# Stack rows interleaved over the partitions, and the scatters of the first batches spread over the attention's last events

## What is computed

```
def _attn(q_in, k_in, v_in, wq, bq, wk, bk, wv, bv, wo, bo, causal):
    Q = (q_in @ wq + bq).reshape(Bq, Sq, H, HD)
    Kp = (k_in @ wk + bk).reshape(Bq, Sk, H, HD)
    V = (v_in @ wv + bv).reshape(Bq, Sk, H, HD)
    scores = jnp.einsum('bqhd,bkhd->bhqk', Q, Kp) / jnp.sqrt(jnp.float32(HD))
...
    a = jax.nn.softmax(scores, axis=-1)
    o = jnp.einsum('bhqk,bkhd->bqhd', a, V).reshape(Bq, Sq, Dm)
    return o @ wo + bo
...
x = _layernorm(x + _attn(x, x, x, ..., True), ln1_g, ln1_b)
x = _layernorm(x + _attn(x, encoder_output, encoder_output, ..., False), ln2_g, ln2_b)
x = _layernorm(x + _moe(x, router_w, router_b, e_w1, e_b1, e_w2, e_b2), ln3_g, ln3_b)
```

## Time and profile before

| | |
|---|---|
| median of 3 runs | 1187.5 us (1185.99 to 1188.43) |
| the profiled execution | 1185.79 us, of which the span 1183.9 us |
| mean granted TensorE clock | 0.938 |
| busy: TensorE matmul, weight load | 1041.1 us (88%), 597.6 us (50%) |
| busy: VectorE, ScalarE, GpSimd | 558.8 us (47%), 588.9 us (50%), 306.5 us (26%) |

### The profile page before, as it was taken

How to read it: one execution, slowest core, us unless ns; L and a number is a source line. 1 busy time by engine, 2 the same in 40 slices (tenths; PEclk the granted TensorE clock), 3 DMA queues, 4 the chain that set the end, 5 groups by cost and what they waited for, 6 DMA issues and landing times. The chain is left out here.

```text
span 1183.9 us, 19018 instructions
## 1 busy us (share of the span) xinstructions
PE 1041.1 (88%) x6318; PEld 597.6 (50%) x6319; DVE 558.8 (47%) x905; ACT 588.9 (50%) x1199; POOL 306.5 (26%) x416
## 2 busy tenths in 40 slices
PE   3889889999999998998998998975429999999976
PEld 1544445333335533343432333321329999999965
DVE  2441467775665576665674754740321121111116
ACT  1246344675764575765565665654143334444422
POOL 5533532404105603003223030243021111111104
PEclk8989889999999999999999998996759999999988
DMA  7985466208209304107507042011031203323324
GB/s 191 130 125 81 69 78 75 43 2 100 37 2 132 57 2 62 20 2 105 154 1 81 1 55 27 1 55 54 30 101 53 98 27 111 106 102 115 107 86 141
DMA packets 71069, 83.41 MB, mean 70 GB/s; under 512 B 10592, under 2 KB 64608, under 8 KB 70880
## 3 DMA queue, kind: packets, MB, share of 16 engines
q1 hardware_dynamic: 63328, 63.17, 30.9%
q0 software_dynamic: 5504, 17.34, 4.6%
q10 hardware_dynamic: 2176, 2.10, 0.5%
HBM read 38.63 MB, written 12.10 MB: 43 GB/s over the span
## 5 line engine op out<-in xcount | busy, mean ns | idle before, releaser
L1101 DVE TENSOR_REDUCE max_q<-v_slot 128x1 f32<-128x1024 f32 (+3 forms) x352 | 399.7, 1172 | 185.0 <-PE v_slot L929 121.5
L1059 ACT ACTIVATE probs<-a_bank 128x512 f32<-128x512 f32 (+1 forms) x688 | 362.6, 591 | 219.8 <-PE a_bank L956 139.8
L956 PE MATMUL a_bank<-q_stack_cross,k_stack_cross 99*128 99x512 bf16 x512 | 172.9, 399 | 26.8 <-issue 11.7
L929 PE MATMUL v_slot<-k_stack_cross,q_stack_cross 96*128 96x512 bf16 x512 | 155.7, 390 | 10.0 <-DMA q_stack_cross<-parts 8.8
L1441 ACT ACTIVATE hidden<-a_bank,b 128x128 f32<-128x128 f32 x216 | 79.4, 368 | 153.2 <-PE a_bank L1389 139.2
L971 PE MATMUL o_bank<-probs,v_cross 128*32 128x512 f32 x1024 | 141.9, 627 | 9.2 <-issue 3.8
L956 PEld LDWEIGHTS a_bank<-q_stack_cross,k_stack_cross 99*128 99x128 bf16 x512 | 47.4, 99 | 167.4 <-ACT probs L1059 86.9
L1397 PE MATMUL v_slot<-stack_or_weights,hidden 128*128 128x256 f32 x576 | 130.3, 379 | 0.0
L1397 PEld LDWEIGHTS v_slot<-stack_or_weights,hidden 128*128 128x128 f32 x576 | 106.7, 190 | 13.0
L1389 PE MATMUL a_bank<-x_col,stack_or_weights 128*128 128x128 f32 x864 | 109.6, 277 | 1.6 <-issue 1.6
L1389 PEld LDWEIGHTS a_bank<-x_col,stack_or_weights 128*128 128x128 f32 x864 | 106.3, 194 | 3.8 <-issue 2.0
(11 more groups left out here) (217 smaller groups left out, 1186.1 us busy)
## 6 DMA issues: line engine op xcount, KB each, us to landing
stack_or_weights<-in_e_w SPq DMA_DIRECT2D x16, 1024.0 KB, 7.8
stack_or_weights<-parts SPq DMA_DIRECT2D x96, 128.0 KB, 5.9
k_stack_cross<-parts SPq DMA_DIRECT2D x96, 128.0 KB, 5.9
q_stack_cross<-parts SPq DMA_DIRECT2D x48, 128.0 KB, 6.4
x_slots<-slots_in SPq DMA_DIRECT2D x38, 129.0 KB
ctxt<-in_ctxT POOLq DMA_DIRECT2D x4, 1024.0 KB, 10.6
xt<-in_xT POOLq DMA_DIRECT2D x4, 512.0 KB, 6.8
xres<-in_x POOLq DMA_DIRECT2D x4, 512.0 KB, 4.4
```

Of the source, the lines that this page charges most:

```text
L929: last = nc.tensor.matmul(slot[:, half * S:(half + 1) * S], lhs, k_stack[1][0:KR, G * u + j, half * S:(half + 1) * S], start=True, stop=True)
L956: last = nc.tensor.matmul(bank[:, i * cols:(i + 1) * cols], lhs, q_stack[kind][0:KM, G * u + j, q0:S], start=True, stop=bool(kind))
L1059: nc.scalar.activation(probs[tile % 2][:, js[0]:js[-1] + 1, q0:S], a_bank[at % AS][:, 0:len(js) * (S - q0)].rearrange("p (j t) -> p j t", ...
L1101: nc.vector.tensor_reduce(most, rows, X, ALU.max, negate=True).then_inc(v_free, 1)
```

## The change

**Interleaved rows.** The row of group g and feature d of a stack moves from partition 16 g + d to partition 6 d + g. A transfer still writes 16 partitions, now every sixth one of the 96, instead of 16 neighbouring ones. Number, size and order of the transfers are the same.

**Scatters one by one.** The event `scatter` becomes 24 events, each with one indirect transfer. The first is put behind the first weighing after `place`, and one more behind each further weighing; what is left when the list ends goes to its end. The waits for slots and rows stand before the first; the wait for landing stands behind the whole list. GpSimd has no part in a weighing.

```
-        last = max(self.order.index(("max_parts", len(UNIT_LIST) - 1)), self.order.index(("place",)))
-        self.order.insert(last + 1, ("scatter",))
+
+        rows = [("scatter", t, k) for t in range(LAST_BATCH) for k in range(2)]
+        spread, started = [], False
+        for ev in self.order:
+            spread.append(ev)
+            started = started or ev == ("place",)
+            if started and ev[0] == "weigh" and rows:
+                spread.append(rows.pop(0))
+        self.order = spread + rows
...
-                                sp.dma_start(stack[g * HD:(g + 1) * HD, h0:h0 + 8, t0:t0 + S], parts[no % 2][:, part, :]).then_inc(stack_in[s], 16)
+                                sp.dma_start(stack[g:KR:NG, h0:h0 + 8, t0:t0 + S], parts[no % 2][:, part, :]).then_inc(stack_in[s], 16)
...
                 elif k == "scatter":
-                    pool.wait_ge(slots_ready, 2)
-                    pool.wait_ge(kept, NO.ln[B - 2, 1] + 1)
-                    for t in range(LAST_BATCH):
-                        for kk in range(2):
-                            pool.indirect_dma_start(out=slots_dram, out_offset=bass.IndirectOffsetOnAxis(ap=early.slot_i[:, kk, t:t + 1], axis=0),
-                                                    in_=x2_all[:, t, :], in_offset=None).then_inc(scattered, 16)
-                    pool.wait_ge(scattered, 16 * 2 * LAST_BATCH)
+                    t, kk = ev[1:]
+                    if t == 0 and kk == 0:
+                        pool.wait_ge(slots_ready, 2)
+                        pool.wait_ge(kept, NO.ln[B - 2, 1] + 1)
+                    pool.indirect_dma_start(out=slots_dram, out_offset=bass.IndirectOffsetOnAxis(ap=early.slot_i[:, kk, t:t + 1], axis=0),
+                                            in_=x2_all[:, t, :], in_offset=None).then_inc(scattered, 16)
+            pool.wait_ge(scattered, 16 * 2 * LAST_BATCH)
```

## The result

| | before | after |
|---|---|---|
| median, same job | 1187.97 us (1185.99 to 1191.55, 4 runs) | 1131.66 us (1130.4 to 1136.96, 4 runs) |
| profiled execution, its span | 1185.79 us, 1183.9 us | 1130.4 us, 1128.5 us |
| mean granted TensorE clock | 0.938 | 0.965 |

The ratio is 0.9531 (95% interval 0.9493 to 0.957). The forecast was 1139 us with a range of 1120 to 1165. Behind the changed list of events (line 172) a line of after is 7 further down than in before, the restacking's line too (L737 is L744).

What follows compares the result with a forecast made beforehand. The prediction took TensorE's own queue in the attention to set the pace. From the profiled execution, 1185.8 - 27 (gaps) - 9 (clock) - 11 (scatters) = 1138.8 us, said as 1139, range 1120 to 1165.

Steps and rivals of the forecast that it cites:

- TensorE's gaps: TensorE's waits in the attention tied to restacking transfers, 30.1 us in sum: a gain of 27 us, bounds 15 and 30.
- nearly all of it can go: Of the 30.1 us of TensorE's waits tied to restacking, each at most 4.7 us, nearly all disappears: 27 us taken.
- The transfer: A restacking transfer's landing falls from 5.9 to 2.3 us, bounded below by the output's transfer at 2.1 us.
- rivals 4 and 5: Restacking transfers get no faster, only the scatters' part gains, 1175 us (chance 0.05); or they get slower, 1231 us (chance 0.07).
- The clock: TensorE's clock falls after restacking waits would go: a gain of 9 us, bounds 3 and 15.
- seven stretches at 1.2 GHz: Stretches around TensorE's restacking waits where the clock falls to its lower level; the shortfall adds up to 37.5 us.
- the half of 37.5: Where TensorE is the limit, half of the time at the lower clock is lost: 18.7 us at most.
- The scatters in unit 31: Breaking up the run of 24 scatters beside unit 31's weighings gains 11 us of 20.8 lost, bounds 0 and 20.8.
- What I kept: Loss left in unit 31 with twelve scatters in a row: 7.1 us, and 3 for the clock.
- The end of the list: The seven late scatters' wait for landing hides behind the routing's matmuls: cost 0, up to 1 us.
- the forecast's own sign: In the profile after, the step into the second part comes no later than 0.5 us after VectorE's last logits.
- The five early scatters: Five scatters behind `place`, done before GpSimd is next needed: cost 0, up to 4 us if TensorE suffers from them.

Runs made afterwards that it cites:

- the third job: A batch of executions with before beside it at 1188.41 us (7 runs); the kernel after, run again in it unchanged, took 1133.78 us.
- the second job: A batch of executions with before beside it at 1168.88 us (9 runs), testing another spread of the rows, paced scatters and added plain transfers.
- the kernel of the second job with twelve scatters in a row: The kernel after, but restacking transfers write every second partition of a range of 32 instead of every sixth of 96: 1130.27 us (2 runs).
- the paced kernel of the third job: The kernel after, but with all 24 scatters paced by weighings, the first ones too, and none behind the last norm: 1122.51 us, ratio 0.9455.

## Why the prediction was right, and where it was off

- **TensorE's gaps: 27 us, measured 27.0** (idle time up to the last weighing of unit 30, 51.2 to 24.3). The step "nearly all of it can go" held: the waits on `parts` and `max_t` are gone and ScalarE took up little.
- **The transfer: 2.3 us, measured 2.4**, with 146 GB/s at share 0.54. The row on which it rested, the output's transfer over 128 partitions, was the right neighbour, with some luck: it differs in more than its partitions, as it is twice the size and writes to memory and not to a stack. That the partitions are what counts was shown afterwards, by the runs that change nothing else. By rivals 4 and 5 it would have stayed at 5.9 or grown.
- **The clock: 9 us, measured 20.4.** This term was mis-sized, beyond its bound of 15. I had counted seven stretches at 1.2 GHz, 37.5 us; the records of before hold ten between 30 and 788 us, 54.6 us together, and those of after two, 6.8 us. The profiled execution of the same kernel in the third job tells the parts of the miss. There all seven that I counted are gone, and the three that I hadn't (17.1 us in before) stand as they were, though the restacking waits are gone; TensorE's busy time up to the last weighing of unit 30 is 690.66 us, 16.6 less than in before. That is 0.9 of the half of 37.5 where I took 0.5: nearly everywhere in those stretches TensorE itself was the limit. The other 3.8 us of the 20.4 belong to this one execution of after, in which most of the three went as well, and which is the fastest of its four; that part is luck.
- **The scatters in unit 31: 11 us, measured 11.6.** That the run of scatters is the cause, a coincidence in time only in the forecast, is now shown by five placings (24, 19, 12 and 10 in a row, and paced); in the second job it had no effect at all. How it holds TensorE up is not shown. What I kept (10 of 20.8 us for twelve) was 9.2. The 20.8 and the 9.2 are both 1.3 us too high, as the undisturbed pace had been taken as 8 times 2.56; the gain is their difference and doesn't suffer. The 11 us were a guess between 0 and 20.8, so that it came so close is partly luck.
- **The end of the list: 0 us, measured +4.6.** This step failed. The text had the last scatter landed at 853.9, 0.2 us before the others reach the end. Three terms were missing: the seven took 9.73 us instead of 8.9 (784.71 to 794.44; one of them 1.89 us beside VectorE's y_cross), the landing 3.0 us from the issue instead of 2.4, and GpSimd's drain, 3.02 us, begins only behind its last wait. So the second part started 5.1 us behind the last logits, where the forecast's own sign was 0.5. I had asked who waits for the landing, but not what GpSimd's queue still does after it. The drain was in the trace of before, in GpSimd's queue at 842.5, hidden by 11 us of other engines' work.
- **The five early scatters: 0, up to 4.** Nothing lost in after; ten in the same place lost 3.6.
- The sum: -27.0 - 20.4 - 11.6 + 4.6 - 1.0 = -55.4 us. The two misses, 11.4 us too little gain and 4.6 us of loss unseen, partly cancel; the forecast of 1138.8 is 8.4 us above the profiled execution. With the second one seen and the clock as forecast it would have been 1143.

Where the edit's second half is judged by itself, it gave back two fifths of what it won (4.6 of 11.6), and in a job without the hold-up it should only cost: there is nothing to win, and the drain is late. Before and after weren't compared in such a job with this edit alone.

## What to carry to other kernels

A transfer's set of partitions is a tuning knob of its own: the same bytes in the same pieces landed in 2.4 instead of 5.9 us when 16 rows spread over more of the partition range, and with the waits went most of the falls of TensorE's clock, worth 0.6 to 0.8 of the waits again. When work moves to the end of an engine's queue, count what that engine must still do behind it: its last wait and its drain become everybody's if it arrives last. Long runs of indirect transfers are best broken up and paced by an event of the engine that must not be disturbed, and kernels that differ in them are compared within one job alone.

## What the runs showed of the hardware that was not expected

In a run of scatters the others learn late that TensorE's matmuls are done. Timeline of before, TensorE's last matmuls ahead of the long stall, and ScalarE's next exponential:

```profile
802.57 1.46 PE L956 MATMUL a_bank<-q_stack_cross,k_stack_cross 99*128 99x512 bf16 x3
...
812.02 0.60 ACT L1059 ACTIVATE probs<-a_bank 128x512 f32<-128x512 f32 x1 [10.40 <-remote]
```

By the profile the matmuls end at 804.03; ScalarE, which waits for them, starts at 812.02, released by something that the profile can't place ("remote"). In the records the first increment of their semaphore behind them stands at 812.00, 8.0 us after the last of them has ended, and with ScalarE's probabilities late TensorE has nothing to do ("issue"). The weighing in front of them, 802.64 at its end, has its increment at 810.58. In after such a delay is 3.5 us at most. In the kernel of the second job with twelve scatters in a row none is over 0.3 us.

Three things bound what this shows. The end of a matmul is modelled, so the records can't tell a late increment from a matmul that was itself done late. The records outside the second job lack increments: after holds 143 of the 384 that 24 scatters make and lacks a few of TensorE's own, so the pairing is uncertain by one or two. And they lack them in the paced kernel of the third job too (254 of 384), which lost nothing, while in the second job they are complete; so gaps in the records go with the job and not with the loss. The scatters' own packets take 182 ns in before and in the second job alike, so their data are not slowed down. Which part is congested, and why one job hasn't it, stays open: no run separates it further.

TensorE's clock can take back what a removed wait has given. Of the six changed placings with every scatter ahead of the last norm, three went through the last projection at 2.4 GHz (24.5 us from the last weighing to the second part), one lost 2.2 us to a fall of the clock there, and two 3.8 (6.4 us for the sixteen matmuls instead of 3.72). One of these two had just come back from a fall (it ended at 766, the next began at 780), the other had not (full from 738 to 772); so what decides isn't shown, and 2 to 4 us of such a comparison belong to no edit.
